# Three edge passes of a graph network: ten gather slots instead of five, index tiles staged two iterations ahead

## The reference, cut to what matters

```python
# layer 0: message of an edge, maximum over the edges of a node
h   = relu(concat([x[dst], x[src] - x[dst]]) @ W1 + b1)
out = segment_max(h @ W2 + b2, dst)              # 0 where a node has no edge
# layer 1: mean of edge_attr by src, then two dense layers
v_e = segment_sum(edge_attr, src) / max(count, 1)
out = relu(relu(concat([x, v_e, u]) @ W1 + b1) @ W2 + b2)
# layer 2: mean of the sources' features by dst, a gate, a dense layer
h   = segment_sum(x[src], dst) / max(deg, 1)
# layer 3: typed attention with 4 heads of 16
a   = sum(kw[src, etype] * qw[dst, etype]) * pri / 4
out = segment_sum(m[src, etype] * softmax_by_dst(a), dst) @ Wa[ntype]
```

## Time and profile before

| | us |
|---|---|
| three runs: lowest, median, highest | 21,959.0, 21,960.2, 21,966.2 |
| profiled execution, span | 21,982.3 |
| pass b, pass c, pass d | 4782, 4362, 4780 |
| preparation, phase a up to pass b | 6288 |
| stages over nodes and table building | 414, 936, 420 |

### The profile page before, as it was taken

The page is one execution under the profiler, slowest core; times in us unless marked ns, Lnnn a source line. Parts: engine busy times, 40 slices in busy tenths (PEclk is TensorE's granted clock), DMA queues, the critical chain, the costliest instruction groups (busy, mean ns, idle before and its releaser), DMA issues. The chain is left out here.

```text
span 21982.3 us, 148548 instructions
## 1 busy us (share of the span) xinstructions
PE 4774.0 (22%) x30182; PEld 4149.9 (19%) x30182; DVE 6911.8 (31%) x16401; ACT 1772.2 (8%) x6281; POOL 15097.0 (69%) x13304
## 2 busy tenths in 40 slices
PE   4444444444423333333320000000041000000002
PEld 4444444444412222222210000000031000000001
DVE  3333333333312222222241111111122444444444
ACT  1111111111100000000010000000021000000001
POOL 5888888888876666666657777777724666666664
PEclk8555555555555555555555555555576555555555
DMA  4444444444422222222231111111122222222222
GB/s 93 53 52 52 52 52 53 50 53 52 52 48 65 65 65 65 63 65 64 65 59 48 47 47 46 47 47 46 43 68 89 87 89 89 87 90 87 89 89 38
DMA packets 1456154, 1380.95 MB, mean 63 GB/s; under 512 B 777810, under 2 KB 1260924, under 8 KB 1455996
## 3 DMA queue, kind: packets, MB, share of 16 engines
q0 software_dynamic: 775408, 541.25, 17.1%
q1 hardware_dynamic: 662716, 736.98, 10.3%
q10 hardware_dynamic: 18000, 102.41, 1.1%
HBM read 762.18 MB, written 617.56 MB: 63 GB/s over the span
## 5 line engine op out<-in xcount | busy, mean ns | idle before, releaser
L500 POOL DMA_INDIRECT agg<-sums,ag_idx x3125 | 4984.9, 1595 | 1166.4 <-issue 1118.5
L534 POOL DMA_INDIRECT gat<-tab_t,gi x3125 | 3021.6, 967 | 1752.5 <-issue 928.0
L534 POOL DMA_INDIRECT gat<-tab_b,gi x3125 | 3014.6, 965 | 1752.6 <-issue 931.3
L534 POOL DMA_INDIRECT gat<-tab_x,gi x3125 | 3299.2, 1056 | 1100.9 <-issue 1061.1
L842 PE MATMUL bank<-at,same 128*128 128x64 f32 x6250 | 1882.7, 431 | 3281.7 <-issue 1057.3
L842 PEld LDWEIGHTS bank<-at,same 128*128 128x128 f32 x6250 | 1570.5, 311 | 3419.7 <-issue 1813.5
L908 PE MATMUL pair<-ident,tails 128*64 128x128 f32 (+1 forms) x20 | 4.9, 419 | 9304.2 <-DVE tails L1209 4931.4
L908 PEld LDWEIGHTS pair<-ident,tails 128*64 128x64 f32 (+1 forms) x20 | 3.0, 167 | 9305.2 <-DVE tails L1209 4931.6
L1302 DVE TENSOR_TENSOR run_sb<-p,gat 128x320 f32<-128x320 f32 x625 | 317.1, 507 | 3710.6 <-DMA gat<-tab_x,gi 3710.6
L1164 DVE TENSOR_TENSOR run_sb<-p,bank 128x320 f32<-128x320 f32 x625 | 304.9, 488 | 3177.7 <-remote 2346.6
L876 PE MATMUL bank<-ident,ub 128*128 128x128 f32 x1250 | 413.0, 434 | 3494.1 <-DVE ub L1192 2228.1
(11 more groups left out here) (263 smaller groups left out, 13806.5 us busy)
## 6 DMA issues: line engine op xcount, KB each, us to landing
edge<-start_rows SPq DMA_DIRECT2D x250, 800.0 KB
run<-run_sb SPq DMA_DIRECT2D x250, 800.0 KB
run<-run_sb SPq DMA_DIRECT2D x125, 900.0 KB
start_rows<-zeros ACTq DMA_DIRECT2D x125, 800.0 KB, 3.5
at<-in_edge_attr SPq DMA_DIRECT2D x125, 800.0 KB
tab_t<-trow SPq DMA_DIRECT2D x98, 512.0 KB, 2.6
agg<-sums,ag_idx POOLq DMA_INDIRECT x3125
gat<-tab_b,gi POOLq DMA_INDIRECT x3125
```

The costliest lines, as they stand in the source:

```text
L500: pool.indirect_dma_start(agg_d[r], rows(agg_d[r], ag_idx[:, k, r:r + 1]), sums[:, k, r, :], None, bounds_check=AGR - 1, oob_is_err=True, ...
L534: pool.indirect_dma_start(gat[:, k, s, 0:width], None, table, rows(table, gi[tp][:, s, k:k + 1])).then_inc(g_in[c][k], 16)
```

## The change

- POOL has ten slots of gathered rows, KS for even and KS for odd iterations. In b and c they are the ten halves of gat (gslot); in d, where a row is twice as wide, gat serves the even iterations and the tile side (free after the scatters) the odd ones. The wait for a slot goes ten steps back instead of five.
- The index tile gi is staged by an instruction of its own, with its own semaphore gi_st, for iteration t+2 at the end of ACT's iteration t. ct and pn are staged where they were. src_i and t_idx get KS more columns of padding.
- The landing semaphores are by slot, ten in all, shared by the three passes, with counts that run on (landed).
- Before the gathers of pass d POOL waits until all scatters have landed, since they read side.
- SP's loads and stores stay as they are.

```diff
-        g_in = {c: [sem(f"{c}_gat{i}") for i in range(KS)] for c in "bcd"}
+        g_in = [[sem(f"gat_in{i}{k}") for k in range(KS)] for i in range(2)]
+        gi_st = sem("gi_staged")
+        def turns(tp):
+            return (T + 1 - tp) // 2
+        EDGES = {"b": 0, "c": 1, "d": 2}
+        def landed(c, t, tp):
+            return t * (8 * SUB) + ((16 if tp == 0 else 8) * SUB + EDGES[c] * turns(tp) * 16 * SUB)
+        def gslot(c, tp, k):
+            if c == "d":
+                half = gat[:] if tp == 0 else side[:, 0:2 * KS * SUB, :].rearrange(
+                    "p (k s a) f -> p k s (a f)", k=KS, s=SUB)
+                return half[:, k]
+            return gat[:].rearrange("p k s (a f) -> p (k s a) f", a=2)[:, (tp * KS + k) * SUB:(tp * KS + k + 1) * SUB, :]
...
-            def gathers(c, table, width, staged, per, used):
+            def gathers(c, table, used):
                 def body(t, tp, first):
-                    pool.wait_ge(staged, (t + 1) * per)
+                    pool.wait_ge(gi_st, t + (EDGES[c] * (T + 2) + 1))
                     pool.nop(nofuse=True)
                     for k in range(KS):
                         if not first:
-                            pool.wait_ge(used, t * KS + (k - KS + 1))
+                            pool.wait_ge(used, t * KS + (k - 2 * KS + 1))
                             pool.nop(nofuse=True)
+                        out_rows = gslot(c, tp, k)
                         for s in range(SUB):
-                            pool.indirect_dma_start(gat[:, k, s, 0:width], None, table,
-                                                    rows(table, gi[tp][:, s, k:k + 1])).then_inc(g_in[c][k], 16)
-                each_iteration(pool, body)
+                            pool.indirect_dma_start(out_rows[:, s, :], None, table,
+                                                    rows(table, gi[tp][:, s, k:k + 1])).then_inc(g_in[tp][k], 16)
+                body(0, 0, True)
+                body(1, 1, True)
+                with loop(pool, 2, T - 1, 2) as t:
+                    body(t, 0, False)
+                    body(t + 1, 1, False)
+                body(T - 1, 0, False)
...
-            gathers("d", tab_t, 2 * F, d_st, 3, d_wm)
+            pool.wait_ge(scat, 2 * 16 * NT)
+            gathers("d", tab_t, d_wm)
...
+            def stage_index(index, t, tp):
+                act.activation(gi[tp][:], index[:, :, bass.ds(t * KS, KS)], ACT.Copy).then_inc(gi_st, 1)
-            def stage(c, st, index, t, tp, with_pen):
+            def stage(st, t, tp, with_pen):
                 cs = bass.ds(t * KS, KS)
-                act.activation(gi[tp][:], index[:, :, cs], ACT.Copy).then_inc(st, 1)
                 act.activation(ct[tp][:], cont[:, :, cs], ACT.Copy).then_inc(st, 1)
...
             def phase_b(t, tp, first):
...
-                        stage("b", b_st, src_i, t + 1, 1 - tp, True)
+                        stage(b_st, t + 1, 1 - tp, True)
+                stage_index(src_i, t + 2, tp)
             def phase_c(t, tp, first):
                 if not first:
                     act.wait_ge(c_s, t * KS)
-                stage("c", c_st, src_i, t + 1, 1 - tp, False)
+                stage(c_st, t + 1, 1 - tp, False)
+                act.wait_ge(c_s, t * KS + KS)
+                stage_index(src_i, t + 2, tp)
```

More of the change, by code:

```diff
@@ L115, in gnn_program @@
         side = sb("side", [P, NT, F])
-        src_i = sb("src_i", [P, SUB, CL + KS], I32)
-        t_idx = sb("t_idx", [P, SUB, CL + KS], I32)
+        src_i = sb("src_i", [P, SUB, CL + 2 * KS], I32)
+        t_idx = sb("t_idx", [P, SUB, CL + 2 * KS], I32)
         cont = sb("cont", [P, SUB, CL + KS])
@@ L416, in edge_io @@
                 for tp in range(2):
-                    sp.wait_ge(r_out[c][tp], 16 + 16 * ((T + 1 - tp) // 2))
+                    sp.wait_ge(r_out[c][tp], 16 + 16 * turns(tp))
             def carry_out(n, car, width):
@@ L512, in to_starts @@
                     for tp in range(2):
-                        pool.wait_ge(e_in["b"][tp], 16 * ((T + 1 - tp) // 2))
+                        pool.wait_ge(e_in["b"][tp], 16 * turns(tp))
                 for i in range(SUB):
@@ L548, in node_rows @@
                 for tp in range(2):
-                    pool.wait_ge(r_out[tag][tp], 16 + 16 * ((T + 1 - tp) // 2))
+                    pool.wait_ge(r_out[tag][tp], 16 + 16 * turns(tp))
                 pool.wait_ge(k_out, 32 * (n + 1))
@@ L557, in node_rows @@
                         batch(b + i, i)
-            gathers("b", tab_b, F, b_st, 3, b_u)
+            gathers("b", tab_b, b_u)
             node_rows("1", run0, car0, F, 0)
             pool.wait_ge(n_out["1"], 16 * NBAT)
-            gathers("c", tab_x2, F, c_st, 2, c_s)
+            gathers("c", tab_x2, c_s)
             node_rows("2", run2, car2, F, 1)
@@ L640, in _ @@
             act.wait_ge(a_done, 1)
-            stage("b", b_st, src_i, 0, 0, True)
+            stage_index(src_i, 0, 0)
+            stage_index(src_i, 1, 1)
+            stage(b_st, 0, 0, True)
             def phase_b(t, tp, first):
@@ L696, in _ @@
             act.wait_ge(n_use["1"], NBAT)
-            stage("c", c_st, src_i, 0, 0, False)
+            stage_index(src_i, 0, 0)
+            stage_index(src_i, 1, 1)
+            stage(c_st, 0, 0, False)
             def phase_c(t, tp, first):
@@ L735, in _ @@
                                        ACT.Copy).then_inc(ta3, 1)
-            stage("d", d_st, t_idx, 0, 0, True)
+            stage_index(t_idx, 0, 0)
+            stage_index(t_idx, 1, 1)
+            stage(d_st, 0, 0, True)
             def phase_d(t, tp, first):
@@ L751, in phase_d @@
                             act.wait_ge(d_acc, t * KS)
-                        stage("d", d_st, t_idx, t + 1, 1 - tp, True)
+                        stage(d_st, t + 1, 1 - tp, True)
+                stage_index(t_idx, t + 2, tp)
             each_iteration(act, phase_d)
@@ L1168, in phase_b @@
             def phase_b(t, tp, first):
-                v.wait_ge(b_st, t * 3 + 3)
+                v.wait_ge(b_st, t * 2 + 2)
                 v.wait_ge(e_in["b"][tp], sides(t, tp))
@@ L1187, in phase_b @@
                         run_max(*back)
-                    v.wait_ge(g_in["b"][k], t * (16 * SUB) + 16 * SUB)
+                    v.wait_ge(g_in[tp][k], landed("b", t, tp))
                     v.wait_ge(b_a, n + 1)
@@ L1292, in phase_c @@
             def phase_c(t, tp, first):
-                v.wait_ge(c_st, t * 2 + 2)
+                v.wait_ge(c_st, t + 1)
                 v.wait_ge(r_out["c"][tp], sides(t, tp))
@@ L1300, in phase_c @@
                     v.wait_ge(c_t1, n + 1)
-                    v.wait_ge(g_in["c"][k], t * (16 * SUB) + 16 * SUB)
-                    TT(run_view(tp, F)[:, :, k, :], p1[:], gat[:, k, :, 0:F], ALU.add).then_inc(c_s, 1)
+                    v.wait_ge(g_in[tp][k], landed("c", t, tp))
+                    TT(run_view(tp, F)[:, :, k, :], p1[:], gslot("c", tp, k), ALU.add).then_inc(c_s, 1)
             each_iteration(v, phase_c)
@@ L1370, in phase_d @@
             def phase_d(t, tp, first):
-                v.wait_ge(d_st, t * 3 + 3)
+                v.wait_ge(d_st, t * 2 + 2)
                 v.wait_ge(e_in["d"][tp], sides(t, tp))
@@ L1389, in phase_d @@
                     v.wait_ge(d_q, n + 1)
-                    v.wait_ge(g_in["d"][k], t * (16 * SUB) + 16 * SUB)
-                    TT(pr[:], gat[:, k, :, 0:F], cur[:], ALU.mult).then_inc(d_pr, 1)
+                    v.wait_ge(g_in[tp][k], landed("d", t, tp))
+                    TT(pr[:], gslot("d", tp, k)[:, :, 0:F], cur[:], ALU.mult).then_inc(d_pr, 1)
                     if back:
```

4 lines of the change are left out of this document (2 added, 2 removed).

## The result

The kernel after takes 22,351.4 us (median; 22,312.7 to 22,362.3), the one before 21,960.1 us beside it: ratio 1.0173, 95% interval 1.0158 to 1.0187, **391 us slower**. The profiled execution has a span of 22,358.2 us, against 21,982.3. The forecast was 22,000; the outcome lies within the wide range and outside the forecast's own (21,930 to 22,200).

The account below looks back on a forecast made before the run. It took a backlog behind POOL's gathers and SP's transfers, worked off at a fixed rate, as the limit. 21,960 + 38 (index tiles) + 2 (scatter wait), other terms 0, gave 22,000 us; range 21,500 to 22,400, the forecast's own 21,930 to 22,200.

Parts of the forecast that it names:

- the second rival: Starts of POOL's bursts in b and d: longer pauses, 16.6 us with three steps left; +300 to +620 us; chance 0.13.
- the mechanism of the forecast: Passes b and d: a backlog behind POOL, worked off at a fixed rate, keeps the pace; 21,930 to 22,200 us, chance 0.58.
- The index tiles: Passes b and d: copy for t+2 after ACT's last step delays POOL's restart; +38 us, far end +930.
- Ten slots: Passes b and d: at most 1639 us of waits removed, but DVE held by POOL's issuing is late next; 0 taken.
- Rival 1: Slots were the limit; POOL runs b and d at c's steady pace, -775 us to 21,185; below 21,300 had chance 0.16.
- The budget of gathers and transfers: Gathers and SP's transfers as fixed-rate work: 35.1 us an iteration in c, 38.2 in b or d; pauses drain it.
- Pass c: No buffer wait to lose, something behind POOL sets the pace; 0, bounds -30 and +30 us.
- The wait for the scatters: Before pass d, POOL's gathers stand behind the scatters' landing; +2 us.
- The layout: Gather slots in b, c and d: row sizes and DVE operand sizes and counts stay; 0.
- The waits about the same sum: Sign of the forecast: POOL's waits for DVE and ACT fewer but longer, sum 1500 to 1800 us.
- Bursts of 75: Sign of the forecast: POOL issues 75 gathers or more between pauses.
- "Remote" waits in b: Sign of the forecast: DVE's waits in pass b with no releaser on record, not below 2300 us.

Follow-up runs that it names:

- E10: Kernel after, held chip: b's index copy after the third step, c's stores twice, d's index copy one step later; 22,193.3 us against 22,103.6 for the kernel before.
- E2: Kernel after with the index tile copied one step later in passes b and d, free chip; ratio 1.0002 to the kernel before.
- E7: Same kernel as E2, run again on a free chip; ratio 1.0002 to the kernel before.
- E11: Kernel before, held chip: three slots in b, 20 tiny ACT copies an iteration in c, loads twice in d; 22,057.3 us against 22,150.2.
- E12: Kernel before with three gather slots instead of five in all passes, held chip; 21,624.9 us against 22,142.7, ratio 0.9764.
- E3: Kernel before with three gather slots instead of five, free chip; ratio 1.0000.
- E4: Kernel before with b's loads and c's and d's stores each issued twice, free chip; ratio 1.0001.
- E9: Same kernel as E4, run again on a free chip; ratio 1.0002.
- E1: Kernel after with GpSimd copying each index tile itself instead of ACT, free chip; 20,246.6 us against 19,886.5 for the kernel before, ratio 1.0181.

## Why the prediction was right and wrong

- **The total** came out slower, as forecast, by 391 us instead of 40; all but some 100 us of that is in pass b. That it lies in the wide range is owed to the room left there for the second rival (above 22,200: 0.13) and not to the mechanism of the forecast, which failed; the sign was in part luck, with 0.35 for slower against 0.31 for faster.
- **The index tiles, +0.15 us an iteration (+38 us),** is the term that was mis-sized. Measured: 286 / 125 = 2.3 us in b, 20 / 125 = 0.16 in d. "Mostly DVE is partway through the iteration when POOL stops" holds in d. In b each cycle ends in the same place, with the held step, three free ones and ACT's part before the restart, and so 18.1 us of pause at each of 61. That is the second rival (16.6 us with three steps left), in one pass of two; its signs, pauses of 16 us and a pass above 4850, are there in b and not in d. The prediction also let a pause come once in three iterations or more; it came once in two. With 5 us more of pause in two iterations the rival's own reckoning gives 2.5 us an iteration, near the 2.3 measured. I had given it 0.13 although I had written that "in b it is worse". E10 shows the place: the copy two steps earlier takes b back.
- **Ten slots, 0.** Right, for a reason half wrong. DVE held by POOL's issuing is what uses up the lead, as written. In d the steps by the timeline are 10.0, 15.3, 15.4, 14.0 us in a row, against 11.0, 15.5, 15.3 in the earlier trace rows. Rival 1 (-775 or more) fails: on a held chip b with ten slots and the early index tile is no shorter than with five (E10), on free ones POOL never waits anyway (E2, E7).
- **The budget of gathers and transfers** ("35.1 us of work in an iteration of c, 38.2 in one of b or d", "not lost time") is wrong. Stores twice cost 11 us of 475 (E10), loads twice about 60 of 390 (E11), and with three slots d needs 36.0 us an iteration (4499 / 125) and b 37.3: the equal 38.2 was chance, and pauses did hold lost time, since less of them gave 518 us (E12). Without POOL's named waits b and d take nearly the same in every kernel: 3962 and 3961 us before, 3950 and 3982 after, 4020 and 3954 with three slots, and 3974 and 3986 on a free chip, where there are none. So in b and d the pauses are, within some 60 us, the whole loss of a held chip; no work queued behind POOL has to be paid in them. I had put b and d side by side, found them 2 us apart and taken it for a law.
- **Pass c** 0: -7, with 351 us for 251 gathers. Right, and "behind POOL" too; but what fills is not SP's transfers.
- **The wait for the scatters,** +2: the stage from c to d is 936 us as before; 0. **The layout** 0: no sign of it in c (-7); in d it can't be told from the 20.
- **Not forecast:** the stages behind b and d, +35 and +26 us. Twice the lead leaves DVE more steps to do after POOL's last gather, where the node stage waits for the last store.
- "The waits about the same sum, 1500 to 1800": 1105 + 818 = 1923, as b's pauses grew. Bursts of 75: they were of 50. "Remote" waits in b, not below 2300: 2708.
- The page "SBUF — State Buffer", section "Who interferes with whom", of the Trainium skill has PE and ACT never wait on anyone; it speaks of the ports of SBUF. As to durations the trace agrees: a copy of E11 that starts late takes 0.21 us, like the index copy of the earlier trace rows. The late starts, one in 1.4 us instead of one in 0.24 while POOL gathers, are something that it doesn't cover.

**Open:** what makes the hold, and why only some chips have it. The runs exclude SP's transfers and the number of ACT's signals as what sets its size; they fit something that takes 1.40 us for a gather which POOL issues in 1.25, and lets other engines through once a gather while it is behind (c: 351 us for 250 gathers). That is an inference. A cause was not isolated, since no run changed the gathers themselves. Nor was the chip told from other properties of a set of runs, which shared one chip each. Two slots, and three slots with later or earlier index tiles, weren't run.

One rival stands untested, the recording of the profile itself. On held chips the traces lack most of the signals (semaphore updates); on free ones they are nearly whole. The DMA table shows it: the second line, of E3, has a time to landing (2.4 us), the first, of the kernel before, has none, since landings are missing.

```profile
gat<-tab_x,gi POOLq DMA_INDIRECT x3125
gat<-tab_x,gi POOLq DMA_INDIRECT x3125, 2.4
```

Counted in the traces, pass c has 6373 signals in the kernel before and 53,465 in E3. E11, where the program makes 2500 more, has 6331: about 1.4 per us in both held traces, whatever is made, and only about the first 12 us of the pass are whole. The hold and the loss go together in every edge pass of these traces. In preparation and phase a signals are missing too (6.9 landings per us on record against 9.1), and these stages take the same time on both kinds of chip (6288 and 6298 us), so a loss alone doesn't slow the kernel. Which causes which, or whether a third thing causes both, no run tells, since each run on record comes with a span and clock from such a recording. It also means that on held chips "remote" may only be a signal that isn't on record, and a named releaser is less sure than elsewhere; the start times and the ratios don't depend on it.

## What to carry to other kernels

When a consumer is slow only while the producer runs, more slots need not help and a later restart can hurt: look at how far on the consumer is when the producer stops, and at which step it may start again. Then try fewer slots, too. And when a wait ends with two signals, the name in the profile is the last of them: the constant reach from signal to start (here 0.90 to 0.91 us) tells which one is the gate. And look whether the trace holds all signals before its named waits are trusted.

## What the hardware showed that I had not expected

- The same kernel takes 19,880 us on two chips and 21,960 to 22,150 on the others: 10 to 11% with the same instructions; DVE's, PE's and ACT's busy times agree within 4% pass by pass, and the difference is in when they start. Passes b, c and d run at 3974, 3929 and 3986 us (E3, whose total is that of before) instead of 4782, 4362 and 4780. What is best on one chip (three, five or ten slots alike) is not so on the other (three of the numbers tried).
- On a held chip an engine with no tie to GpSimd, ACT's extra copies in E11, falls to one instruction per gather, after ten to twelve at full speed in each iteration.
- A whole 800 KB load or store more in each iteration cost nothing on free chips (E4, E9); on held ones a store cost 0.09 us (E10) and a load some 0.5 us, 0 to 1 (E11).
- On held chips a trace keeps about 1.4 signals per us in pass c where a free chip's keeps 13.6 (the kernel before and E11 against E3).
- A copy of an index tile (128 partitions, 25 columns) on GpSimd costs 0.96 us in its path, with its waits (E1), where ACT's takes 0.21.
